# Layer norm of a transformer block divided: the mean taken from a transposed input, the deviation applied to the products

## The reference

```
xn = (x - mean(x)) / sqrt(var(x) + 1e-5)
Q = elu(xn @ wq.T + bq) + 1;  K = elu(xn @ wk.T + bk) + 1;  V = xn @ wv.T + bv     (16 heads of 32)
att = (Q @ (K.T V)) / (Q @ sum(K) + 1e-8) @ wo.T + bo                              (linear attention)
w   = top 2 of 8 experts from sigmoid(xn @ W_router) + bias, normalised
gate = xn @ W_gate + shared LoRA + expert LoRAs weighted by w;   up likewise       (1376 columns)
ffn = (silu(gate) * up) @ W_down + shared LoRA + expert LoRAs weighted by w
out = x + att + ffn
```

## Time and profile before

| | us |
|---|---|
| median of 3 runs | 672.68 (672.13 to 672.84) |
| profiled execution | 672.65 |
| its span, first to last instruction | 670.9 |
| TensorE busy | 659.6 |
| VectorE busy | 376.2 |
| ScalarE busy | 258.2 |
| GpSimd busy | 127.2 |

### The profile page before, as it was taken

How to read it: one execution, slowest core, us unless ns; L and a number is a source line. 1 busy time by engine, 2 the same in 40 slices (tenths; PEclk the granted TensorE clock), 3 DMA queues, 4 the chain that set the end, 5 groups by cost and what they waited for, 6 DMA issues and landing times.

```text
span 670.9 us, 10347 instructions
## 1 busy us (share of the span) xinstructions
PE 659.6 (98%) x3568; PEld 545.3 (81%) x3568; DVE 376.2 (56%) x698; ACT 258.2 (38%) x413; POOL 127.2 (19%) x290
## 2 busy tenths in 40 slices
PE   6899999999999999999999999999999999999998
PEld 6788999977777788888888888888888888888886
DVE  5577888768775956344345443445444336534433
ACT  4334455467235324323233333343233324323321
POOL 3456666636246230000000000000000000000000
PEclk9999999999999999999999999999999999999999
DMA  7966666644764679960025100012500002300001
GB/s 226 327 198 218 192 218 219 235 177 143 304 220 141 245 226 2 4 201 0 0 79 193 58 0 0 0 65 77 188 0 0 0 0 78 126 0 0 0 0 63
DMA packets 41642, 74.21 MB, mean 111 GB/s; under 512 B 19392, under 2 KB 20288, under 8 KB 39952
## 3 DMA queue, kind: packets, MB, share of 16 engines
q1 hardware_dynamic: 38672, 64.52, 35.8%
q10 hardware_dynamic: 2736, 9.05, 3.5%
q0 software_dynamic: 208, 0.30, 0.3%
HBM read 52.81 MB, written 21.04 MB: 110 GB/s over the span
## 4 chain that ended last, share of the span: by engine, by line
PE 90%; DVE 4%; issue 2%; POOL 2%; DMA 1%; ACT 1%; POOLq 0%; DVEq 0%; ACTq 0%
PE bank L1238 20%; PE bank L1239 19%; PE bank L1240 19%; PE bank L1483 18%; PE bank L1456 6%; DVE den L1084 2%; PE bank L1469 1%; PE bank L1467 1%; DMA w_raw<-in_wkT 1%; PE bank L1257 1%; PE bank L1269 1%; PE bank L1356 1%; PE bank L1494 1%; PE bank L1496 1%; PE bank L1278 0%
## 5 line engine op out<-in xcount | busy, mean ns | idle before, releaser
L1238 PE MATMUL bank<-x,up_h 128*128 128x512 f32 (+1 forms) x352 | 137.3, 390 | 0.2 <-DVE x3r L1049 0.2
L1239 PE MATMUL bank<-x,up_h 128*128 128x512 f32 (+1 forms) x352 | 137.1, 390 | 0.0
L1240 PE MATMUL bank<-x,up_l 128*128 128x512 f32 (+1 forms) x352 | 137.1, 390 | 0.0
L1175 DVE TENSOR_TENSOR hf<-bank,silu 128x512 f32<-128x512 f32 x44 | 30.4, 691 | 155.0 <-issue 135.3
L1483 PE MATMUL bank<-dn,hid_h 128*128 128x512 f32 x352 | 108.9, 391 | 0.0
L669 ACT ACTIVATE hid_h<-hf 128x512 fp32r<-128x512 f32 x44 | 27.8, 632 | 144.1 <-DVE hf L1175 144.1
L1238 PEld LDWEIGHTS bank<-x,up_h 128*128 128x128 f32 x352 | 66.1, 188 | 14.4 <-issue 0.7
L1483 PEld LDWEIGHTS bank<-dn,hid_h 128*128 128x128 f32 x352 | 65.9, 188 | 14.5 <-DVE res L1200 0.6
L1240 PEld LDWEIGHTS bank<-x,up_l 128*128 128x128 f32 x352 | 66.1, 188 | 13.7
L1239 PEld LDWEIGHTS bank<-x,up_h 128*128 128x128 f32 x352 | 66.1, 188 | 13.6
L880 DVE TENSOR_TENSOR up_l<-up_raw,up_h 128x1024 fp32r<-128x1024 f32 x44 | 55.0, 1249 | 28.1 <-ACT up_h L669 28.1
(11 more groups left out here) (166 smaller groups left out, 1082.3 us busy)
## 6 DMA issues: line engine op xcount, KB each, us to landing
x<-scr_x SPq DMA_DIRECT2D x7, 2048.0 KB, 8.7
up_raw<-in_ffn_up SPq DMA_DIRECT2D x11, 768.0 KB, 7.2
scr_x<-xt ACTq DMA_DIRECT2D x16, 512.0 KB, 4.9
xin<-in_x SPq DMA_DIRECT2D x16, 256.0 KB, 5.1
scr_z<-zt SPq DMA_DIRECT2D x16, 256.0 KB, 2.1
x3r<-in_x SPq DMA_DIRECT2D x16, 256.0 KB, 3.5
scr_att<-x3r SPq DMA_DIRECT2D x16, 256.0 KB, 2.8
z<-scr_z SPq DMA_DIRECT2D x4, 1024.0 KB, 4.9
```

Source lines behind the costliest of these rows:

```text
L1175: nc.vector.tensor_tensor(hf[:], ps_u[:], silu[:], ALU.mult).then_inc(h_done, 1)
L1238: nc.tensor.matmul(dst, lh, rh, start=start, stop=False, **kw)
L1239: nc.tensor.matmul(dst, lh, rl, start=False, stop=False, **kw)
L1240: return nc.tensor.matmul(dst, ll, rh, start=False, stop=stop, **kw)
```

## The change

The layer norm is taken apart. With r = 1/sqrt(var + eps), xn @ W = r × ((x − mean) @ W), so r can be applied to results.

- A transposed copy of x comes as a further input xT (same values, laid out by tile on the host). SyncE loads it into xtr (two buffers) beside x (load_xt). transpose_tokens is gone. mean_rows(t, s) has TensorE transpose the column of means, broadcast to 128×128: one instruction in place of four, whose result holds the mean of token n in column n of every row. It stands after the value products of tile t−2. centre (VectorE) subtracts it from xtr, in place of normalise. tokens_hi and tokens_lo read xtr (SBUF) instead of ps_xt (PSUM).
- GpSimd makes rs (r), nrs (−r) and keeps r in rstd for all tiles: two instructions more for each tile; rstd_of(t+2) instead of (t+3).
- In stage 1 kb becomes a scalar_tensor_tensor with rs; vf's activations have scale rs, rexp's scale nrs.
- The scratch tensor scr_x now holds the centred x. Queries: query_scaled (VectorE) multiplies ps_q by r, broadcast over partitions in rb, into qf; the relus read qf. r travels through a new DRAM scratch scr_r (a store of 2048 single values after tile 15) and broadcast loads (load_rb). TensorE's queries wait for query_scaled instead of the relus. VectorE's order for groups 0 and 1 is rewritten.
- FFN: gate_scaled (VectorE) multiplies the gate by r into silu, ScalarE's silu works in place, TensorE's next gate waits for gate_scaled. The up side isn't scaled; results multiplies ps_out by r instead.
- The loads of stage 2 are spread over tiles 1 to 3 instead of standing together after tile 0; statistics of tiles 0 and 1 come first on VectorE; more matmuls on the identity fill the start (8 for 4).

```diff
@@ sync
+            def load_xt(t, s):
+                wait(sp, xtl_done, t - 1)
+                sp.dma_start(xtr[:, s:s + 1].rearrange("p o k n -> p o (k n)"),
+                             dram["xT"][:, bass.ds(t, 1)].rearrange("p o k n -> p o (k n)")).then_inc(xtr_in[s], 16)
+            def load_rb(dst, g, done, n=1):
+                sp.dma_start(dst, scr_r[:, g * GN:(g + n) * GN].to_broadcast([P, n * GN])).then_inc(done, 16)
             load_x(0, 0)
             sp.dma_start(ident[:], dram["ident"]).then_inc(ident_in, 16)
+            load_xt(0, 0)
+            load_x(1, 1)
...
+                if t == TILES - 1:
+                    sp.wait_ge(rstd_done, TILES)
+                    sp.dma_start(scr_r.rearrange("e (t p) -> p (e t)", p=P), rstd[:], allow_slow_non_contiguous=True).then_inc(scr_rd, 16)
+            sp.wait_ge(scr_rd, 16)
+            load_rb(rb[0][:], 0, rb_in[0])
             sp.wait_ge(k_ready, TILES)
             x3_load(1)
@@ gpsimd, rstd_of
-                nc.gpsimd.tensor_tensor(rstd[:], vare[:], mhalf[:], ALU.pow).then_inc(ln_rstd, 1)
+                nc.gpsimd.tensor_tensor(rs[:, s:s + 1], vare[:], mhalf[:], ALU.pow).then_inc(rs_done, 1)
+                pool.wait_ge(rs_done, t + 1)
+                nc.gpsimd.tensor_tensor(nrs[:, s:s + 1], rs[:, s:s + 1], minus[:], ALU.mult).then_inc(ln_rstd, 1)
+                nc.gpsimd.tensor_tensor(rstd[:, bass.ds(t, 1)], rs[:, s:s + 1], one[:], ALU.mult).then_inc(rstd_done, 1)
@@ scalar, query_relus
-                act.wait_ge(q_ready, n + 1)
+                act.wait_ge(qs_done, n + 1)
@@ scalar, chunk
-                act.wait_ge(g_ready, n + 1)
-                nc.scalar.activation(silu[:], ps_g[:], ACT.Silu).then_inc(silu_done, 1)
+                act.wait_ge(gs_done, n + 1)
+                nc.scalar.activation(silu[:], silu[:], ACT.Silu).then_inc(silu_done, 1)
@@ vector
-            def normalise(t, s):
+            def centre(t, s, uses):
+                dve.wait_ge(xt_ready, t + 1)
+                dve.wait_ge(xtr_in[s], 16 * (uses + 1))
+                nc.vector.tensor_tensor(xtr[:, s], xtr[:, s], ps_xt[:, s * P:(s + 1) * P].unsqueeze(1).to_broadcast([P, KD, P]),
+                                        ALU.subtract).then_inc(ln_done, 1)
@@ vector, order of groups 0 and 1
-            queries(0, (0,))
+            for par in range(2):
+                dve.wait_ge(scr_xd[par], 16 * TILES // 2)
+            query_scaled(0, 0)
             key_values(TILES - 1, TILES // 2 - 1)
             heads_of(1)
-            queries(0, (1,))
+            queries(0, (0,))
+            query_scaled(0, 1)
             lora_weighted(TILES - 1, (TILES - 1) % 2)
             lora_lo(TILES - 2)
-            queries(0, (2,))
+            queries(0, (1,))
+            query_scaled(0, 2)
             dve.wait_ge(bdnh_done, 1)
             sub(bdn[0:ER, 1], bdn_raw[0:ER, 1], bdn[0:ER, 1]).then_inc(bdn_done, 1)
+            queries(0, (2,))
+            query_scaled(0, 3)
             queries(0, (3,))
             m_lo(0, (0, 1))
             reciprocals(0)
+            query_scaled(1, 0)
             m_lo(0, (2, 3))
             dve.wait_ge(bdn_done, 1)
             reciprocal_lo(0)
+            queries(1, (0,))
+            query_scaled(1, 1)
             scaled(0, (0, 1))
-            queries(1, (0,))
+            queries(1, (1,))
             scaled(0, (2, 3))
-            queries(1, (1,))
+            query_scaled(1, 2)
             kvt_lo(1)
             lora_lo(TILES - 1)
             queries(1, (2,))
+            query_scaled(1, 3)
             m_lo(1, range(KD))
             queries(1, (3,))
@@ vector, FFN
+            def gate_scaled(n, g):
+                dve.wait_ge(g_ready, n + 1)
...
+                nc.vector.tensor_tensor(silu[:], ps_g[:], r, ALU.mult).then_inc(gs_done, 1)
             def chunk(n, c, s, g, last=False, due=None):
                 start = isinstance(n, int) and n == 0
                 if not last and not start:
                     split_up(c + 1, 1 - s, n + 2)
+                gate_scaled(n, g)
                 split_dn(c, s, n + 1)
@@ vector, stage1 and results
-                nc.vector.tensor_tensor(kb[:], ps_k[:], bk_b[:], ALU.add).then_inc(kb_done, 1)
+                dve.wait_ge(ln_rstd, t + 1)
+                nc.vector.scalar_tensor_tensor(kb[:], ps_k[:], rs[:, s:s + 1], bk_b[:], ALU.mult, ALU.add).then_inc(kb_done, 1)
...
-                        nc.vector.tensor_tensor(res[:, j, :], res[:, j, :], ps_out[j][:], ALU.add).then_inc(o_done, 1)
+                        nc.vector.scalar_tensor_tensor(res[:, j, :], ps_out[j][:], r, res[:, j, :], ALU.mult, ALU.add).then_inc(o_done, 1)
@@ tensor
-            def transpose_tokens(t):
+            def mean_rows(t, s):
+                pe.wait_ge(ln_stats, t + 1)
+                wait(pe, ln_done, t - 1)
+                nc.tensor.transpose(ps_xt[:, s * P:(s + 1) * P], mv[:, s, 0:1].to_broadcast([P, P]), ident[:]
+                                    ).then_inc(xt_ready, 1)
@@ tensor, stage1
-                if ahead(t, 1) and not first:
-                    transpose_tokens(t + 1)
+                if first:
+                    mean_rows(1, 1)
                 if s == 0 and behind(t, 2):
                     keys_by_values(t - 2, half - 1, 0)
                     keys_by_values(t - 1, half - 1, 1)
                 wait(pe, va_done, t)
                 tile_of(ps_va, s, va_h[:, :, 0:VA], va_l[:, :, 0:VA], split_before=KD if first else None
                         ).then_inc(va_ready, 1)
-                if first:
-                    transpose_tokens(1)
+                if ahead(t, 2):
+                    mean_rows(t + 2, s)
@@ tensor, queries and gate_or_up
-                    wait(pe, qmax_done, g * KD + c - 1)
+                    wait(pe, qs_done, g * KD + c - 1)
...
-                dst, free, ready = ((ps_g, silu_done, g_ready), (ps_u, h_done, u_ready))[a]
+                dst, free, ready, uses = ((ps_g, gs_done, g_ready, n), (ps_u, h_done, u_ready, n + 1))[a]
```

More of the change, by code:

```diff
@@ L970, in stage1 @@
                 if ahead(t, 2):
-                    normalise(t + 2, s)
+                    centre(t + 2, s, half + 1)
                 dve.wait_ge(vz_ready, t + 1)
@@ L992, in _ @@
             stats_of(0, 0, 0)
-            normalise(0, 0)
+            stats_of(1, 1, 0)
+            centre(0, 0, 0)
+            tokens_lo(0, 0)
             for k in range(KD):
@@ L1119, in group @@
                 if not last:
+                    query_scaled(g + 1, 0)
+                scaled(g, (3,))
+                if not last:
                     queries(g + 1, (0,))
-                scaled(g, (3,))
                 if last:
```

185 lines of the change are left out of this document (115 added, 70 removed).

## The result

| | us |
|---|---|
| kernel before, median of 6 runs | 672.67 (672.13 to 672.89) |
| changed kernel, median of 6 runs | 713.65 (711.56 to 714.97) |
| ratio | 1.060, 95% interval 1.058 to 1.062 |
| changed kernel, profiled execution | 713.82, span 711.8 |

The change makes the kernel 41 us slower. I had said slower, but 698.3 with 706 as the upper end: 15 us too little.

What follows compares the result with a forecast made beforehand. The prediction took TensorE, busy 98% of the span, to bound the kernel. 672.65 us + 11.0 (stage 1) + 10.1 (queries) + 4.5 (FFN) = 698.3, chance 0.60, with a range from 691 − 2 to 705 + 1.

Steps and rivals of the forecast that it cites:

- the start: Start of stage 1: earlier loads cost 0 to 1.5 us, offset by VectorE not stopping for tile 1; nothing in sum.
- the round trip of the deviations: Before the first query scaling: store of 2048 values takes 5 to 7 us, broadcast load 3.5; deviations there at 139.3.
- the work behind it: Group 0 queries up to denominators(0): chained chunks and lora_lo(14), z stores not needed yet; with the round trip +5.1 us.
- denominators(1): Queries of group 1: rr and m_hi late behind ScalarE's query passes; +9.9 us in all, 4.8 of it after denominators(0).
- Stage 1's loop: Stage 1: mean row waits for statistics, kb for TensorE; rows sum to 8.34 us a tile, 8.5 taken; stage +11.0.
- the 0.1 for tokens_lo: Stage 1's loop: tokens_lo, now reading two SBUF tiles beside GpSimd, takes 0.1 us longer (bounds 0 and 0.4).
- GpSimd's own loop: Stage 1: GpSimd's chain from eq through rden and score back to eq comes to 8.3 to 8.8 us a tile.
- the 1.9 that I gave to the mean row: Tile 0 of stage 1: TensorE's wait for tile 2's statistics puts kb(1) at 22.3 instead of 20.39.
- 3.05 + 1.7: Group 0 queries: 3.05 us a chunk without overlap, plus 1.7 where lora_lo(14) waits for ScalarE after exp(0,1).
- a rival said: Query waits: clock falls to 1.2 GHz and doubles some 3 us of products; 701.5 us in all, chance 0.10.
- The FFN: FFN: +1.6 us before gate(1), 0.9 at each of three group borders, +0.2 at the end; +4.5 in sum.
- a loop bound by GpSimd: Rival in stage 1: GpSimd is the bound, 9.0 to 9.2 us a tile, 6 to 8 more; 705 us, chance 0.13.

Runs made afterwards that it cites:

- e1: Changed kernel with TensorE's mean row of tile t+2 put behind the router and LoRA products of tile t; 700.88 us.
- e2: Changed kernel with deviations of tiles 0 to 7 stored in tile 10 and read back for group 0 in tile 12, the others stored after stage 1; 706.50 us.
- e3: Changed kernel with the start in the order of the kernel before (x and statistics of tile 1, tokens_hi and tokens_lo of tile 0 later); 711.59 us.
- e4: Changed kernel with TensorE multiplying the identity 26 times in its wait before query product (0,2) and 14 times before denominators(0); 711.55 us.
- e5: Changed kernel with the edits of e1, e2 and e3 together; 694.54 us.
- e6: As e5, with VectorE's group 0 query list reordered: next query_scaled ahead of the addition, LoRA remainders of tile 14 and down-projection remainder later; 689.12 us.
- e7: Changed kernel without the FFN's scaling of the gate's products by the deviation, a price and no kernel to use; 709.21 us.
- e8: As e6, with neither the gate's products nor the results scaled in the FFN; 683.47 us.
- e9: Changed kernel with deviations of groups 0 and 1 made into rows by TensorE transposes after tiles 10 and 11, the DRAM store serving only later uses; 706.06 us.
- e10: As e6, with two ScalarE swaps: reciprocal rounding of group 0 ahead of query chunk (1,0), m(1) rounding ahead of chunk (1,3); 684.58 us.
- e11: Changed kernel with mean row behind, old start order, rows by TensorE as in e9, VectorE's order of e6 and ScalarE's of e10; 680.08 us.
- e12: As e11, with VectorE's FFN list reordered: chunk 0's gate scaling earlier, results ahead of the second chunk's work at group borders; 675.58 us, ratio 1.0037.

## Why the prediction was wrong

The stretches of the profiled executions, us. The first column is the start of kb of tile 0 and each further one the way to the next start; den. is denominators, FFN the first FFN product.

| | kb(0) | to kb(1) | to kb(15) | to den.(0) | to den.(1) | to FFN | to the end | median |
|---|---|---|---|---|---|---|---|---|
| before | 15.28 | 5.11 | 108.06 | 19.68 | 23.24 | 57.69 | 441.84 | 672.67 |
| after | 19.85 | 6.92 | 116.74 | 32.77 | 30.60 | 58.03 | 446.89 | 713.65 |
| e1 mean row | 19.96 | 5.39 | 105.51 | 32.73 | 30.52 | 58.08 | 446.91 | 700.88 |
| e2 early store | 19.95 | 6.92 | 118.13 | 24.68 | 30.75 | 58.11 | 446.86 | 706.50 |
| e3 old start | 16.98 | 6.91 | 116.73 | 32.78 | 30.51 | 58.06 | 446.93 | 711.59 |
| e4 fill | 18.65 | 6.91 | 116.72 | 33.49 | 29.15 | 58.04 | 446.84 | 711.55 |
| e5 three | 17.54 | 5.37 | 110.09 | 24.70 | 30.24 | 58.08 | 446.88 | 694.54 |
| e6 VectorE | 15.83 | 5.39 | 109.84 | 20.47 | 29.14 | 58.06 | 446.87 | 689.12 |
| e7 no gate scaling | 20.02 | 6.92 | 116.74 | 32.64 | 30.66 | 58.04 | 442.78 | 709.21 |
| e8 no FFN scaling | 17.86 | 5.37 | 108.01 | 20.50 | 27.55 | 58.04 | 441.97 | 683.47 |
| e9 rows alone | 18.27 | 8.45 | 117.60 | 24.70 | 30.58 | 58.05 | 446.85 | 706.06 |
| e10 ScalarE | 17.25 | 5.38 | 107.49 | 20.48 | 24.98 | 58.10 | 446.92 | 684.58 |
| e11 rows | 16.44 | 5.39 | 106.06 | 20.48 | 24.37 | 58.42 | 446.84 | 680.08 |
| e12 FFN | 16.75 | 5.39 | 106.02 | 20.50 | 24.38 | 58.31 | 441.45 | 675.58 |

Most edits move their own column and hardly another, and that is the evidence that the losses are separate. Three things move without an edit: kb(0), by up to 2 us between runs of one start; the late tile 13 behind the early store (e5, e6, e8, e10), by 2 us; and the way from denominators(0) to (1), 1.6 us shorter in e8 than in e6.

The prediction failed at two steps and at what hangs on them: the start (4.5 us), the round trip of the deviations (6.0), the work behind it (2.0) and denominators(1) (2.6). That is 15.1 of the 15.3 us missed.

**Stage 1's loop: right.** The sum from rows was 8.34 us a tile, and 8.33 to 8.37 it took from tile 6 on. The forecast used 8.5, which was too much: the 0.1 for tokens_lo wasn't there (0.68 us beside GpSimd, as alone), and GpSimd's own loop wasn't the bound. The waits before the mean row, 1.36 and about 0.5 us in turn, are the 1.4 and 0.6 foretold. e1 shows the cause by taking it away.

**The start: wrong, 4.5 of the 15.3 us.** kb(0) came 4.6 us late, where I had nothing; the 1.9 that I gave to the mean row between kb(0) and kb(1) was 1.8. The step that failed was "which costs 0 to 1.5 us, but VectorE no longer stops for tile 1 between value weights; I put that at nothing in sum". I compared the loads and left out the queue: statistics of tile 1 now stand ahead of centre(0) on VectorE, so x of tile 1 must have landed before anything of tile 0 can go on. It landed at 9.55, and from there centre, rounding and key weights came one after another, and the first key product at 13.19 instead of 8.96. The old order gives back 2.5 us (e3). A range of 0 to 1.5 for a step whose landing no row showed was no bound. The question to ask is: which load must land before the first product?

The clock fell here too, which I had not seen coming. Windows of 5 us (as in e4) of the changed kernel, behind the wait of 4.4 us:

```profile
10.00:15.00 5.00, 1.81 (x4) 1.49 (x5) 4.26 (x10) 3.92 (x8) 3.91 (x9) 0.60 1.01 365
15.00:20.00 5.00, 5.00 (x20) 4.25 (x19) 3.78 (x8) 2.20 (x5) 0.00 (x0) 0.72 0.53 114
```

From the first key product to the twelfth and last it took 4.75 us, before 2.65. What that costs at kb(1) no run shows: in e9 these products ran at 1.00, and kb(0) came 1.6 us earlier than in the changed kernel, but kb(1) at 26.72, no earlier, with the clock at 0.66 behind a wait of 2.3 us for the mean row. In the runs with the old start and e1's edit, kb(1) comes 11.03 us after the first key product where the clock stayed up (e6, e11, e12) and 11.30 to 11.50 where it fell (e5, e8, e10).

**The round trip: the mechanism right, its size wrong, 6.0 us.** query_scaled(0,0) was put 10.9 us behind kb(15) and came 16.8 behind it. I scaled the 40.3 us store of 16384 values down by count, to 5 to 7 us for 2048; it took 11.3. The load took 5.1, not 3.5. Scaling a duration down through zero leaves out the part that doesn't shrink. e2 and e9 take the round trip off the path by two ways, and both gain 8.1 us up to denominators(0). The Trainium skill (DMA: Bandwidth & Descriptors, § Rules for kernel authors) says that a non-contiguous last dimension becomes one descriptor for each element. The trace agrees; the DMA packets between 143.8 and 155.3 us, in which the store of 2048 values is the only one of its kind:

```profile
DMA packets 2210, 0.30 MB, mean 26 GB/s; under 512 B 2080, under 2 KB 2080, under 8 KB 2208
```

**What stood behind it: wrong, 2.0 us up to denominators(0).** I wrote that SyncE's wait holds up z stores "which are not needed yet". One was: ScalarE waits 0.82 us at 167.13 for the z store of tile 13 before it makes zt of tile 14, for which VectorE waits 3.03. In e2 and e9, where SyncE isn't held up, ScalarE has no such wait and VectorE waits 2.10. The chunk with that wait took 5.75 us where I had 3.05 + 1.7. The other three took 3.4, 3.3 and 3.5 instead of 3.05: relu started 0.7 to 0.8 us after the scaling and exp 1.25 after relu, where I had 0.62 and 1.13. The lower clock isn't in it: with the clock up (e4) the way from the first scaling to denominators(0) took the same time, but for the longer wait for zt. That most of this chain needn't be waited for at all shows in e6, which takes 4.2 us off by order alone.

**denominators(1): 2.6 us more than the 4.8 foretold.** The order was read rightly: I named the same two instructions as e10, rr behind the passes of (1,0) and m_hi behind those of (1,3), and moving them gives back 4.2. In e4 the stretch is 1.45 us shorter with the clock up; the rest wasn't taken apart.

**The clock: it fell, as a rival said, but as an extra.** Five of the six windows of 10 us between 150 and 210 us have 0.74 to 0.92 where before all had 1.00. The rival priced 3 us; e4 puts it at 1.45, all of it behind denominators(0), and at 2 at most. The Trainium skill (TensorE: Matmul & The Clock Gate, § What's actually happening) has an idle TensorE put back to half clock; the trace agrees, behind waits of 4.4 and 6.8 us. Up to denominators(0) the slower products cost nothing, because there VectorE's chain ends last.

**The FFN: right.** 1.60 us before gate(1) and 0.92, 0.92 and 1.00 at the borders, against 1.6 and 0.9 foretold. The form of the results costs nothing there (e7). The added scalings cost nothing by themselves: four of the 44 stood in front of something urgent, and with their places changed the stretch takes 441.45 us (e12), 0.4 less than before the change.

**The range.** Its upper end, 706, came from a loop bound by GpSimd. The two steps that failed, the start and the round trip, had a value but no rival of their own. I had weighed the steps whose rows I had and not those whose rows were missing.

## What to carry to other kernels

When an instruction moves to another engine's queue, follow two things: what must be ready for it, and what stands behind it. Five times here a wait of a few us came from one instruction ahead of more urgent ones, and by the stretches 29 of 41 us went by putting it elsewhere (12.7 mean row, 2.5 start, 4.2 VectorE's and 4.2 ScalarE's order in the queries, 5.4 FFN). Another 8.1 went with the round trip through DRAM. Cut two traces at the same few starts and compare stretches; then one edit should move one stretch, and a stretch that moves without an edit tells how far two executions differ. Where a step rests on a transfer that no row shows, give it a wide bound and a rival, and don't scale a store of single values by its count alone.

## What the runs showed of the hardware

- A store of 2048 single values landed 11.3 us after its issue (11.4 in e1, 11.0 in e4), though it carries 8 KB; the window around it holds 2080 packets under 512 bytes. Beside one of 1024 values the loads of x landed after 8.8 us instead of 4.3 (e2), and the tile that needed them came 1.4 to 4.3 us late (e2, e5, e6, e8, e10). A later issue on SyncE's queue took 2.13 us instead of 0.35 in e5, but 0.74 and 0.78 in e6 and e10.
- GpSimd and VectorE disturb each other, and in these rows GpSimd pays. GpSimd's groups from 40 to 120 us, the tie product and the power, first before, then after (busy, mean ns):

```profile
L603 POOL TENSOR_TENSOR eq<-eq,earlier_sb 128x64 f32<-128x64 f32 x11 | 3.6, 323 | 14.3 <-DVE eq L918 14.3
L581 POOL TENSOR_TENSOR rstd<-vare,mhalf 128x1 f32<-128x1 f32 x11 | 6.0, 548 | 0.9
```

```profile
L659 POOL TENSOR_TENSOR eq<-eq,earlier_sb 128x64 f32<-128x64 f32 x9 | 6.3, 702 | 18.0 <-DVE eq L976 18.0
L634 POOL TENSOR_TENSOR rs<-vare,mhalf 128x1 f32<-128x1 f32 x9 | 8.9, 988 | 0.7
```

  The same instructions take about 0.4 us longer where tokens_lo or kf, VectorE instructions of two SBUF inputs, run beside them; these keep their 0.68 us. Each time VectorE's had started first, by 0.16 and 0.11 us. Before, the product ran beside a tokens_lo with one input in PSUM, and the power beside no VectorE instruction. In the earlier trace rows it was VectorE that paid, beside long GpSimd additions.
- A TensorE that had waited 6.8 us came back at 1.2 GHz (granted clock 0.50 from 161 to 164 us): the next products started 0.43 us apart, and 0.23 after 164.65. It was the same behind the waits of 4.4 us in the start and before denominators(0). Multiplying the identity in the two waits of the queries kept it at 2.4 GHz (e4).
